# Cross-attention and top-2 expert layer: expert work of 14 of 16 tiles moved into one-expert jobs of 128 gathered rows, with a new order inside the attention slots

## The reference

```python
x = x + xattn(layernorm(x), ctx, seg_id, ...)   # 16 heads of 128+64, latent widths 96 (q) and 64 (kv)
x = x + ffn(layernorm(x), gate_w, gate_b, expert_w, expert_b)

# xattn: a query at segment s sees keys s-8 .. s only; softmax; values; W_o
# ffn, 8 experts, 2 per token:
gate_logits = einsum('nsd,de->nse', x, gate_w) + gate_b
_, top_idx  = top_k(gate_logits, 2)
all_out     = relu(einsum('nsd,edo->nseo', x, expert_w) + expert_b)
out         = take(all_out, top_idx).mean(axis=2)
```

## Time and profile before

| | us |
|---|---|
| median of three runs | 450.7 |
| the profiled execution | 450.26 |
| its span, first to last instruction | 448.4 |
| PE busy | 422.8 |
| DVE, ACT, POOL busy | 260.5, 288.2, 265.8 |
| first scores (group 0), scores of group 7, scores of group 63 start at | 35.5, 78.3, 417.0 |

### The profile page before, as it was taken

How to read it: one execution, slowest core, us unless ns; L and a number is a source line. 1 busy time by engine, 2 the same in 40 slices (tenths; PEclk the granted TensorE clock), 3 DMA queues, 4 the chain that set the end, 5 groups by cost and what they waited for, 6 DMA issues and landing times.

```text
span 448.4 us, 9783 instructions
## 1 busy us (share of the span) xinstructions
PE 422.8 (94%) x2574; PEld 317.6 (71%) x2574; DVE 260.5 (58%) x1153; ACT 288.2 (64%) x940; POOL 265.8 (59%) x363
## 2 busy tenths in 40 slices
PE   2967999999999999999999999999999999999995
PEld 2836676777777777777777777777777777777663
DVE  2657757565656565655656565656565565656341
ACT  1225676776676767676767667676767676766633
POOL 4034556576565657574757656575757475765555
PEclk9968999999999999999999999999999999999998
DMA  9990000000000000000000000000000000000001
GB/s 214 273 376 36 2 1 2 1 1 2 12 2 14 1 15 0 12 0 12 0 12 0 0 12 0 12 0 12 0 12 0 12 0 13 1 1 13 0 12 31
DMA packets 16529, 12.54 MB, mean 28 GB/s; under 512 B 7568, under 2 KB 16128, under 8 KB 16240
## 3 DMA queue, kind: packets, MB, share of 16 engines
q1 hardware_dynamic: 13488, 10.64, 8.1%
q10 hardware_dynamic: 2880, 1.43, 1.4%
q0 software_dynamic: 128, 0.09, 0.1%
HBM read 10.04 MB, written 2.10 MB: 27 GB/s over the span
## 4 chain that ended last, share of the span: by engine, by line
PE 81%; POOL 4%; issue 3%; DVE 3%; ACT 2%; DVEq 0%; POOLq 0%; ACTq 0%
PE psum L544 18%; PE psum L545 12%; PE psum L546 12%; PE psum L875 11%; PE psum L961 8%; PE psum L913 7%; PE psum L885 6%; PE psum L943 4%; ACT prob L1006 1%; POOL q_sb L1045 1%; DVE xn L471 1%; POOL acc L1074 1%; POOL acc L1071 1%; PE psum L440 1%; PE psum L552 1%
## 5 line engine op out<-in xcount | busy, mean ns | idle before, releaser
L1097 POOL TENSOR_TENSOR prob<-prob,prec 128x512 f32<-128x512 f32 x64 | 68.4, 1069 | 83.5 <-DVE prec L1231 83.5
L1006 ACT ACTIVATE prob<-nsc,nmax 128x128 f32<-128x128 f32 x256 | 99.7, 395 | 0.0
L1045 POOL TENSOR_TENSOR q_sb<-rope_a,rope_b 128x256 f32<-128x256 f32 x64 | 47.0, 734 | 57.8 <-DVE rope_b L1160 57.7
L875 PEld LDWEIGHTS psum<-kT_all,qT 128*128 128x128 f32 x512 | 68.0, 193 | 6.0 <-issue 0.4
L875 PE MATMUL psum<-kT_all,qT 128*128 (+1 forms) x512 | 68.4, 277 | 0.0
L1176 DVE CUSTOM_DVE_ANT_0 nsc<-psum,mask 128x128 f32<-128x128 f32 x256 | 59.2, 286 | 14.9 <-PE psum L875 14.9
L1027 ACT ACTIVATE eout<-psum,gates 128x256 f32<-128x256 f32 x128 | 54.0, 476 | 19.9 <-DVE gates L1240 10.4
L994 ACT COPY qT<-psum 128x512 f32<-128x512 f32 x64 | 37.5, 586 | 43.6 <-PE psum L913 43.6
L544 PE MATMUL psum<-we_hi,xT_hi 128*128 128x512 f32 x128 | 57.3, 448 | 0.0
L1231 DVE RECIPROCAL prec<-psum_h 128x4 f32<-128x4 f32 x64 | 11.4, 178 | 74.6 <-ACT prob L1006 74.6
L546 PE MATMUL psum<-we_hi,xT_lo 128*128 128x512 f32 x128 | 50.4, 394 | 0.0
(11 more groups left out here) (131 smaller groups left out, 863.2 us busy)
## 6 DMA issues: line engine op xcount, KB each, us to landing
wo_raw<-in_w_o SPq DMA_DIRECT2D x2, 1024.0 KB, 10.7
we_raw<-in_expert_w SPq DMA_DIRECT2D x1, 2048.0 KB, 14.4
out<-acc SPq DMA_DIRECT2D x16, 128.0 KB, 1.7
x_all<-in_x SPq DMA_DIRECT2D x2, 640.0 KB, 7.9
ctxT<-in_ctx_t SPq DMA_DIRECT2D x2, 512.0 KB, 7.2
wuqT<-in_w_uq_t ACTq DMA_DIRECT2D x1, 768.0 KB, 13.4
wukT<-in_w_uk_t SPq DMA_DIRECT2D x1, 512.0 KB, 11.3
x_all<-in_x SPq DMA_DIRECT2D x1, 512.0 KB, 13.2
```

The source lines that it names most:

```text
L875: mm = pe.matmul(B_S[r][:, h, :], qT[r][:, h, :], keys, start=True, stop=True)
L1006: e = act.activation(prob[r][:, h, :], nsc[r][:, h, :], ACT.Exp, bias=nmax[r][:, h:h + 1], scale=-1.0, accum_out=psum_h[r][:, h:h + 1])
L1045: pool.tensor_tensor(q_sb[1 - r][:, :, KVC:P], rope_a[1 - r][:], rope_b[1 - r][:], ALU.add).then_inc(m["rope_joined"], 1)
L1097: pool.tensor_tensor(p[:], p[:], prec[r][:, :].unsqueeze(2).to_broadcast([P, HG, P]), ALU.mult).then_inc(m["prob_normed"], 1)
```

## The change

1. **Jobs.** Tiles 0 to 13 (`NS = 14`) are no longer multiplied with all experts. After its top two are known (slot g = 1), a tile's choice goes as `chosen16` through two small bfloat16 matmuls on PE (slot g = 2), which count for each row how many rows before it chose the same expert; seven or eight small DVE instructions (slot g = 3) make of that two places in a DRAM list, and POOL writes the tile's 128 normed rows there by two indirect DMAs (in the slot g = 0 of tile t, for tile t-3). After the last of them DVE makes a table of 35 jobs (`job_table`, 18 instructions up to the row table, most waiting for the one before, on 8 to 245 columns), each 128 rows of one expert. A job: SP reads its row address from the table and loads the rows, PE transposes them, ACT and DVE split them, PE multiplies them with one expert (256 columns), ACT applies relu, and POOL scatters 128 rows to `halves` in DRAM. At the end SP loads both halves (2 x 14 x 128 rows), DVE adds them to `x`, and SP stores the 14 tiles.
2. **Dense tiles last.** Tiles 14 and 15 keep the dense way, in eight pieces after the jobs.
3. **Slot order.** The transposes of the probabilities and the V product lie two slots behind the scores (before: one), the output product three (before: two). The q transposes of group i now start the slot that uses them (before: in the slot ahead, after the output product). The row maxima and the exponentials are signalled in halves: the second half of group i's exponentials stands in slot i+1. The normalisation on POOL and the reciprocal move by a slot too.
4. **Start.** In the preparation block SP, as its last instructions, writes one 128-row padding block to each of eight regions of the list (8 x 132 KB), and POOL makes constants. The walk begins at slot -4.

The core of the diff (of the slots' products one line each).

```diff
+NS = 14
+CAP = NS * P
+ROW = D + 2
+NJ = TPB * NS + NE - 1
...
@@ prep.sync
             sp.dma_start(we_raw[:], expert_w.rearrange("(c p) n -> p c n", p=P)).then_inc(S("ld_we"), 16)
+            sp.wait_ge(S("pad_set"), 2)
+            for e in range(NE):
+                sp.dma_start(slots.ap()[CAP * e:CAP * e + P, :], pad_row[:]).then_inc(S("padded"), 16)
...
@@ main.tensor
+            def job_turn(j):
+                pe.wait_ge(m[f"ld_job{j % 4}"], 16 * (j // 4 + 1))
...
+                at_least(pe, "jx_lo_done", j - 1)
+                for c in range(DC):
+                    mm = pe.transpose(JOB_TURNED[j % 2][:, P * c:P * c + P], wanted[j % 4][:, P * c:P * c + P], ident[:])
+                mm.then_inc(m["jT_done"], 1)
+
+            def job(j):
+                if j == 0:
+                    pe.wait_ge(m["table_done"], 1)
...
+                    job_turn(0)
+                at = pe.value_load(job_cols[0:1, j:j + 1], min_val=0, max_val=O * (NE - 1))
+                if j + 1 < NJ:
+                    job_turn(j + 1)
+                pe.wait_ge(m["jx_lo_done"], j + 1)
+                at_least(pe, "jrelu_done", j - 1)
+                cols = bass.ds(at, O)
+                z = EXPERT_BANKS[j % 2][:, 0:O]
+                pe.matmul(z, ones3[:], bias3[:, cols], start=True, stop=False)
+                for c in range(DC):
+                    mm = mm3(pe, z, jx_hi[j % 2][:, c, :], jx_lo[j % 2][:, c, :], we_hi[:, c, cols], we_lo[:, c, cols],
+                             start=False, stop=(c == DC - 1))
+                mm.then_inc(m["je_done"], 1)
+
             def slot(b, k):
+                if g == 1 and live(t - 2, TILES):
+                        mm = gate_product(pe, c, j)
+                if live(i, GROUPS):
+                        mm = pe.transpose(B_QT[:, P * h:P * h + P], q_sb[r][:, h, :], ident[:])
                 if live(i + 1, GROUPS):
                     mm3(pe, B_Q[:, :], qc_hi[j1][:], qc_lo[j1][:], wq_hi[:, hs, :].rearrange("p h n -> p (h n)"),
+                if live(i - 2, GROUPS):
+                        mm = pe.transpose(B_PT[:, P * h:P * h + P], prob[r][:, h, :], ident[:])
                 if live(i, GROUPS):
                         mm = pe.matmul(B_S[r][:, h, :], qT[r][:, h, :], keys, start=True, stop=True)
                 if g == 0 and live(t - 2, TILES):
+                        mm = pe.transpose(B_E[:, P * c:P * c + P], row[j][:, P * c:P * c + P], ident[:])
+                if g == 2 and live(t - 2, TILES) and gathered(t - 2):
+                    at_least(pe, "chosen", t - 1)
+                    pe.matmul(B_E[:, RANKS:RANKS + NE], before16[:], chosen16[:], start=True, stop=True)
+                    pe.matmul(B_E[:, RANKS + NE:RANKS + 2 * NE], ones16[:], chosen16[:], start=True, stop=True
+                              ).then_inc(m["rank_done"], 1)
+                if live(i - 3, GROUPS):
+                        mm = mm3(pe, B_Y[:, 0:D], oT_hi[1 - r][:, q, :], oT_lo[1 - r][:, q, :], wo_hi[:, 2 * gp + q, :],
+                if live(i - 2, GROUPS):
+                        mm = pe.matmul(B_O[KVC * odd:KVC * odd + KVC, 0:D], v_cur[:], pT[r][:, odd::2, :],
+                if job_slot(i):
+                    job(i - FIRST_JOB_SLOT)
...
@@ main.scalar
+            def job_relu(j):
+                act.wait_ge(m["je_done"], j + 1)
+                at_least(act, f"put{j % 4}", 16 * (j // 4))
+                act.activation(jout[j % 4][:], EXPERT_BANKS[j % 2][:, 0:O], ACT.Relu, scale=0.5).then_inc(m["jrelu_done"], 1)
+
+            def job(j):
+                act.wait_ge(m["jT_done"], j + 1)
+                at_least(act, "je_done", j - 1)
+                act.copy(jx_hi[j % 2][:], JOB_TURNED[j % 2][:, 0:D].rearrange("p (c n) -> p c n", c=DC)
+                         ).then_inc(m["jx_hi_done"], 1)
+                if j > 0:
+                    job_relu(j - 1)
...
@@ main.gpsimd
+                if g == 0 and live(t - 3, TILES) and gathered(t - 3):
...
+                    for high in range(2):
+                        pool.indirect_dma_start(slots.ap(), bass.IndirectOffsetOnAxis(place_i[j][:, high:high + 1], 0),
+                                                row[j][:], None, bounds_check=NE * CAP - 1, oob_is_err=False
+                                                ).then_inc(m[f"sent{j}"], 16)
+            def job(j):
+                pool.wait_ge(m["jidx_done"], j + 1)
+                pool.wait_ge(m["jrelu_done"], j + 1)
+                pool.indirect_dma_start(halves.ap(), bass.IndirectOffsetOnAxis(jidx[j % 4][:, 0:1], 0), jout[j % 4][:], None,
+                                        bounds_check=2 * NS * P - 1, oob_is_err=False).then_inc(m[f"put{j % 4}"], 16)
...
@@ main.vector
+            def job(j):
+                if j == 0:
+                    dve.wait_ge(m["table_step"], 16)
+                dve.wait_ge(m[f"ld_job{j % 4}"], 16 * (j // 4 + 1))
+                at_least(dve, f"put{j % 4}", 16 * (j // 4))
+                dve.tensor_scalar(is_high[j % 4][:], wanted[j % 4][:, D + 1:ROW], job_region[:, j:j + 1], float(NS * P), ALU.is_lt,
+                                  ALU.mult).then_inc(m["is_high_done"], 1)
+                dve.wait_ge(m["jx_hi_done"], j + 1)
+                at_least(dve, "je_done", j - 1)
+                dve.tensor_tensor(jx_lo[j % 2][:], JOB_TURNED[j % 2][:, 0:D].rearrange("p (c n) -> p c n", c=DC),
+                                  jx_hi[j % 2][:].bitcast(F32), ALU.subtract).then_inc(m["jx_lo_done"], 1)
+                dve.wait_ge(m["is_high_done"], j + 1)
+                dve.scalar_tensor_tensor(out=jidx[j % 4][:], in0=is_high[j % 4][:], scalar=job_drop[:, j:j + 1],
+                                         in1=wanted[j % 4][:, D:D + 1], op0=ALU.add, op1=ALU.add).then_inc(m["jidx_done"], 1)
+            def job_table():
+                step = m["table_step"]
+                dve.wait_ge(m["placed"], NS)
+                dve.tensor_tensor(counts[:], filled[:], region[:], ALU.subtract).then_inc(step, 1)
...
+                dve.tensor_tensor(passed[:], job_no[:, :].unsqueeze(2).to_broadcast(shape),
+                                  blocks_to[:, 0:NE - 1].unsqueeze(1).to_broadcast(shape), ALU.is_ge).then_inc(step, 1)
...
+                dve.scalar_tensor_tensor(out=job_row[:], in0=job_last[:], scalar=last_row[:, 0:1], in1=job_skip[:],
+                                         op0=ALU.add, op1=ALU.min).then_inc(m["table_done"], 1)
...
+            def slot(b, k):
+                if isinstance(i, int) and i == GROUPS:
+                    job_table()
+                if g == 3 and live(t - 2, TILES) and gathered(t - 2):
+                    at_least(dve, "rank_done", t - 1)
+                    dve.tensor_tensor(place[:], B_E[:, RANKS:RANKS + NE], filled[:], ALU.add).then_inc(m["place_step"], 1)
...
+                    dve.tensor_tensor(filled[:], B_E[:, RANKS + NE:RANKS + 2 * NE], filled[:], ALU.add).then_inc(m["placed"], 1)
...
@@ main.sync
+                for j in range(TPB):
+                    sp.wait_ge(m[f"sent{j}"], 32 * (NS // TPB))
+                sp.wait_ge(m["table_done"], 1)
+                for j in range(NJ):
+                    at = sp.value_load(job_row[0:1, j:j + 1], min_val=0, max_val=NE * CAP - P)
+                    at_least(sp, "jT_done", j - 3)
+                    at_least(sp, "jidx_done", j - 3)
+                    sp.dma_start(wanted[j % 4][:], slots.ap()[bass.ds(at, P), :]).then_inc(m[f"ld_job{j % 4}"], 16)
+                for j in range(4):
+                    sp.wait_ge(m[f"put{j}"], 16 * len(range(j, NJ, 4)))
+                for n, ts in enumerate(SUM_PARTS):
+                    for h in range(2):
+                        rows = slice(P * (NS * h + ts.start), P * (NS * h + ts.stop))
+                        sp.dma_start(half[h][:, ts, :], halves.ap()[rows, :].rearrange("(t p) d -> p t d", p=P)
+                                     ).then_inc(m[f"ld_half{2 * n + h}"], 16)
+                for n, ts in enumerate(SUM_PARTS):
+                    sp.wait_ge(m["half_added"], 2 * n + 2)
+                    sp.dma_start(out[ts].rearrange("t p d -> p t d"), x_all[:, ts, :]).then_inc(m["sum_stored"], 16)
+                for n in range(TPB):
+                    sp.wait_ge(m["acc_step"], 2 * GPT * (n + 1))
+                    sp.dma_start(out[NS + n], acc[n][:]).then_inc(m[f"out_stored{n}"], 16)
```

More of the change, by code:

```diff
@@ L539, in walk @@
                     slot(b, k)
-            for k in range(SLOTS + 9):
+            for k in range(SLOTS + 6):
                 slot(B - 1, k)
@@ L661, in tile @@
                 for c in range(DC):
-                    mm = pe.transpose(B_X[:, P * c:P * c + P], x2n[:, P * c:P * c + P], ident[:])
+                    mm = pe.transpose(B_X[:, P * c:P * c + P], row[0][:, P * c:P * c + P], ident[:])
                 mm.then_inc(m["g_xT_mm"], 1)
@@ L967, in _ @@
                 walk(pe, slot)
+                for j in range(IN_SLOTS, NJ):
+                    job(j)
```

(19 more changed lines are left out.)

491 lines of the change are left out of this document (296 added, 195 removed).

## The result

The changed kernel takes 437.1 us, the median of four runs (434.16, 435.81, 438.34, 440.62), against 450.7 before: ratio 0.970, 95% interval 0.962 to 0.978. The forecast was 428.0, with an own range of 418 to 438. The profiled execution took 438.34 with a span of 436.5, against the 425.7 that the sum had for the span.

The account below looks back on a forecast made before the run. PE's own work was taken to bound the loop, a third of it experts. From 448.4 us: start +6, groups 0 to 7 -3.6, groups 7 to 63 -93.7, drain +68.6, giving 425.7, as a median 428.0; own range 418 to 438.

Parts of the forecast that it names:

- the signs that I had named for a wrong forecast: A scatter taking over 1.7, DVE idle in every slot, or PE's clock falling in the jobs.
- Start: Preparation block: SP's eight padding issues hold up all engines, +6 us, between +4 and +11.
- Groups 0 to 7: First seven groups: 5.6 us each instead of 6.12, between PE's 5.26 and the old value, -3.6 us.
- Groups 7 to 63: Loop of 14 tiles: 17.5 us a tile, 245 us against 338.7, -93.7 us.
- DVE and PE are then level: Loop: DVE's 17.1 us a tile, idle time before `xT_lo` included, against PE's 16.8.
- Drain, 13 us: Scores of group 63 to first job product: 13 us, with 4.5 for `job_table` and group drains within it.
- Job, 1.9: Each of 35 jobs: PE work 1.35 us plus register read 0.55, 66.5 us in all.
- End, 20.5: After the jobs: dense pieces, relus, additions and store 19.3 us, plus 1 for SP's stores of the sums.
- their rival: Jobs: POOL's scatters bind, 2.6 us a job, +24.5 us, 452.5 us; chance 0.17.
- DVE as the bound of the loop: Rival for the loop: 19 us a tile, or 1.5 more, +21 us, 449 us; chance 0.14.
- quick jobs of 1.35: Rival for the jobs: PE's queue reads the register while matmuls run, 19 us less, 409 us; chance 0.20.
- a start held for 11: Rival for the start: padding issued at the rate the queue drains, 11 us, +5, 433 us; chance 0.07.

Follow-up runs that it names:

- experiment 2: Changed kernel with the eight padding stores issued at the start of the main block instead of in the preparation block: 432.2 us, ratio 0.957.
- Experiment 4: Changed kernel with one more DVE instruction (unread `bn_stats` of 256 columns) in each slot: 441.2 us, ratio 0.979.
- Experiments 3 and 6: 3: changed kernel, `job_table` behind `oT_lo`, reciprocal and `xT_lo`, 435.8 us; 6: the same plus tile 15's root ahead of job 0's scatter on POOL, 430.8 us.
- experiment 10: Changed kernel with plain stores to consecutive rows in place of POOL's job scatters (rows land in wrong places): 430.3 us, ratio 0.954.
- the five moves: Changed kernel with padding later, `job_table` later, tile 15's root first, eight job buffers and dense additions on DVE: 421.1 us, ratio 0.937.
- experiment 12: Kernel with the five moves plus unread q products on PE: five in slot 64, two in job 2, three in job 3: 420.4 us, ratio 0.930.
- Experiment 7: Changed kernel with the sixteen additions of the dense tiles on DVE, between its additions of the halves, instead of on POOL: 435.5 us, ratio 0.966.
- experiment 11: Changed kernel with unread q products on PE: five in slot 64, three in job 1, one in job 3, three in job 4: 439.3 us, ratio 0.977.

## Why the prediction was right and where it failed

The sign was right, and so was the main mechanism: the loop is PE's own work, and it shrinks with the experts taken out. The size was 9 us too good in the medians. That 437.1 still lies within 418 to 438 is in part luck, for it is the difference of two errors, 10.5 too much for the attention part and 21.4 too little for the drain. Of the signs that I had named for a wrong forecast two came: DVE stood idle in the loop, and PE's clock fell in the jobs.

**Start.** Right: +5.2 against +6, and experiment 2 shows that 4.6 of it is these eight issues; of the 4.6 at group 0, 3.6 were left at group 63. In single executions with the same start group 0 stands at 39.7 to 42.4.

**Groups 0 to 7.** 36.6, 5.23 a group: PE's sum of 5.26 alone, without the 0.34 that I put on top for DVE. But with the same code other executions took up to 38.7 (5.53 a group), at a clock of 0.60 from 42 to 50 where this one had 1.00, so part of the 2.6 is this execution's clock.

**Groups 7 to 63.** PE's 16.8 was right (16.99 measured). What failed is "DVE and PE are then level", 17.1 for DVE. By the window it is busy 77% of a tile, 13.1. Idle time before `xT_lo` was no constant of the instruction: it fell from 23.3 to 15.6 in all. And I had carried over busy time that was itself waiting for POOL. The small subtraction `qc_lo` shows it, before and after, by line on DVE:

```profile
L1222 DVE TENSOR_TENSOR qc_lo<-qc_all,qc_hi 96x128 fp32r<-96x128 f32 x16 | 13.7, 856 | 0.5
```

```profile
L1452 DVE TENSOR_TENSOR qc_lo<-qc_all,qc_hi 96x128 fp32r<-96x128 f32 x16 | 5.4, 336 | 0.5
```

The 0.52 more in each was waiting counted as busy, by my reading the block of the earlier trace rows; no run separates it. Experiment 4 settles that PE binds.

**Drain, 13 us.** This is the step that failed first. The table's 4.5 us were right (4.7), and the text even said that it stands ahead of `oT_lo`. It did not follow what stood behind: reciprocal, POOL's normalisation, the scatters, the first loads. I let the last scatters lie beside the table; they stood behind it. Experiments 3 and 6 show the two queue jams: 3.1 us at the first product, 3.5 behind job 0.

**Job, 1.9.** The mean was near (2.08 over all), the reasons wrong. Reading the register does not cost 0.55: without it jobs 7 to 34 take 1.70, with it 1.71 to 1.85, and the shortest of several kernels with the read is 1.33, as without; whether it costs something smaller is not shown. At the clock's upper level a job is 1.79 (experiment 10: 0.27 of it through the scatters), and those until 357 are at the lower level, 2.33 where none waits. The forecast named a falling clock only as what would make it wrong; it should have been a term, because PE had stood idle ahead of `oT_lo`. With the five moves its price up to job 7 is 4.8 us by experiment 12.

**End, 20.5.** 27.8. (The terms, 19.3 and 1, make 20.3.) To the last addition it is 22.3 where the sum had 18.8, and behind it 5.5 where it had a store of 1.7. I took POOL's additions at 0.73 as in the earlier trace rows, while DVE's eight large additions ran beside them, and the earlier trace rows had shown what such a pair does. Experiment 7 took 2.7 of the 7.3 away. Behind the last addition the kernel before needed only 2.4; now SP's stores of the sums, 9.3 us of issues until 429.2, stand ahead of the dense tiles' stores, which the forecast priced at 1. No run tests that part.

**Rivals.** The scatters do not bind at 2.6 a job as their rival had it: 0.97 an instruction, 1.28 apart at the closest. The Trainium skill (SBUF, State Buffer, the box on DVE blocking a GpSimd DMA), cited for a DVE copy that holds up such a DMA to about 3100 ns, does not bear on the jobs as I had used it: the box ties that case to a DVE operation in a two-port mode, such as an SBUF to SBUF copy in float32, and no such copy runs in a job. The issues lasted 974 on average, beside DVE instructions of 0.2 to 0.42. DVE as the bound of the loop is refuted by experiment 4, quick jobs of 1.35 by the table above, and a start held for 11 by its 5.2.

## What to carry to other kernels

When a step is moved ahead on an engine's list, follow everything behind it to its last reader on other engines; here a 4.7 us table and a 0.6 us root each cost over 3 us that way. When work is taken out of a full engine, look for the waits that it had covered: here taking out the experts in the old order gave 20 of the loop's 101 us. And take a tail's durations from instructions that ran beside the partner they will have there, and put a price on every stretch in which PE stands idle, also for what the clock does after it.

## What was not expected of the hardware

- The granted clock went from 1.00 to 0.50 after PE had stood idle 4.68 us at 319 to 324, and stayed there for some 30 us; with that idle time filled (experiment 11) it was 1.00 from 319 to 325, and dipped later (0.77 from 325 to 340).
- POOL's scatter of 128 rows of 1 KB is an instruction of 0.97 us, against 0.55 for a plain store of the same bytes; two stand 1.28 apart at the closest.
- The blocking between POOL and DVE goes both ways: POOL's additions from 0.73 to as much as 1.72, DVE's of 1024 columns from 1.22 (experiment 7) to 1.48 on average.
